# Attention half steps issued tile by tile, with value products in halves, on one Trainium2 core

## Chip, cores and metric

The kernel runs on one core of one Trainium2 chip. The metric is the device time in microseconds, median of the runs of one launch each; the lower the better.

## What is computed

Two layers over x of shape (4, 512, 256), with a context of the same shape. Layer 0: gated cross-attention (16 heads of 16, softmax over 512 context rows), then a top-2 mixture of 8 experts. Layer 1: gated cross-attention again, then a feed-forward block with quantised activations and ternary weights. Cut to the attention and the two blocks after it:

```python
q = split_heads(LN(x) @ Wq.T + bq); k = split_heads(ctx @ Wk.T + bk); v = split_heads(ctx @ Wv.T + bv)
w = softmax(einsum('bhqd,bhkd->bhqk', q, k) / sqrt(16))
x = x + tanh(g_xattn[l]) * (merge(einsum('bhqk,bhkd->bhqd', w, v)) @ Wo.T + bo)
# layer 0: x = x + tanh(g_ffn[0]) * sum over the 2 best experts of wf_e * (LN(x) @ We)
# layer 1: x = x + tanh(g_ffn[1]) * bitlinear(gelu(bitlinear(LN(x), w1)), w2)
```

## The kernel before

Eight passes follow one another, `p` = 0 to 7: four batches of layer 0, then the same four of layer 1. A pass has 16 attention steps `G` (four heads of a group times four tiles of 128 context rows), and a step has two half steps, the slots of the program. `table()` writes one list of work for the whole kernel, slot by slot; each engine walks that list and issues only what it owns, so the list fixes every engine's order. Nothing is decided at run time but the waits on semaphores.

In a slot stand first the tiles of attention, then one "piece" of other work from `work_table()` (a projection, an expert, a part of the feed-forward block), so that TensorE has something to do beside the softmax. The tiles of attention are:

- `S` (`s_pair`, L754): two scores of 128 query rows by 512 context rows, heads r = 0 and 1, six steps ahead of their use. They serve only for the row maxima, which VectorE takes (`maxima`, L1171) from three PSUM buffers `psS`. Head 0 lies on partitions 0 to 63 of the stacks `qs` and `ks`, head 1 on 64 to 127, so the two matmuls use different row halves of the array.
- `T` (`t_pair`, L768): the same scores transposed, with the maxima as two further contraction rows, for the same two heads, into the two buffers of `psT`. ScalarE takes both with one exponential of 1024 columns (`exps`, L991) into `pt`. The next `t_pair` waits for that exponential.
- `PV` (`pv_quad`, L782): in every second slot, four matmuls of 512 columns into `psO`, one for each head of the group, side by side in four strips of 32 columns of the array, fp32. Each is two MATMULs in the trace, so a quad shows x8. It takes the step before, G-1.

The maxima of four steps are copied and split on GpSimd (`m`, L648, L651), transposed on TensorE (`MT`, L791), copied by ScalarE (`mt_`, L1007) and put into rows of `qs` with four small DMAs on the queue of SyncE (`max_rows`, L531). `SPLIT` projects keys or queries (L707); ScalarE writes it twice (`qf` L938, `parts` L939), GpSimd subtracts (L574), and the parts go through DRAM into `qs` and `ks`. `ME` is an expert (L843 to L845, six matmuls in a slot, read by VectorE at L1302). `F1` (L879), `HT` (L889) and `F2` (L897) are the feed-forward block, and GELU (L1042) reads `F1` from `psT` and `psS`; `VV` (L727) is the value projection. After the last pass comes a tail in which one batch goes alone through `OP`, the layer norm, `XB` (L858), `F1`, `HT` and `F2`.

## Time and profile before

| | us |
|---|---|
| median of 3 runs (lowest, highest) | 766.89 (765.59, 769.69) |
| the profiled run's own time | 766.51 |
| its span in the trace | 764.7 |
| outside the span | 1.8 |
| PE busy in the span | 676.7 (88%) |
| DVE busy | 530.5 (69%) |
| ACT busy | 446.8 (58%) |
| POOL busy | 167.0 (22%) |

PE is TensorE, DVE VectorE, ACT ScalarE, POOL GpSimd and SP SyncE, whose busy time is not counted. The ends of matmuls are modelled: a lone matmul of 512 columns is shown with 0.39 to 0.50 us, while the next one of the same kind starts after 0.23. Starts are therefore the better measure. The passes take 85.1, 90.1, 88.8, 88.9, 88.8, 82.1, 76.1 and 78.1 us, counted from first exponential to first exponential; ahead of them lie 46.9 us, behind them 39.8.

### The profile page before, as it was taken

What the parts mean: (1) busy time and instruction counts of PE and PEld (TensorE: products, weight loads), DVE (VectorE), ACT (ScalarE), POOL (GpSimd) and SP (SyncE); (2) the same over time, 40 slices, a digit from 0 to 9 for tenths busy, and PEclk for the clock granted to TensorE, in tenths of its full rate; (3) what the DMA queues carried; (4) which work ended last, traced back from release to release, by engine and by line L of the source; (5) the groups of instructions that cost most, each with busy time, mean ns of one, the idle gap of its engine ahead of it and who ended that gap; (6) DMA issues with size and microseconds to landing.
All of it is one profiled execution on the core that took longest, in us unless ns stands there. A gap on an engine that the chain in (4) does not pass through costs nothing.

```text
span 764.7 us, 10140 instructions
## 1 busy us (share of the span) xinstructions
PE 676.7 (88%) x3550; PEld 323.6 (42%) x3554; DVE 530.5 (69%) x1138; ACT 446.8 (58%) x572; POOL 167.0 (22%) x302
## 2 busy tenths in 40 slices
PE   4799999998999999998999989998889789987746
PEld 2433333344544445444554445443344344432324
DVE  3467876578886688868787688864786768775234
ACT  2227666773346633664336734468776778568746
POOL 6325222630010310121101410113210311021132
PEclk9769999999999999999999999999999999969987
DMA  7848578512120601123220321216032312200000
GB/s 239 230 117 317 180 232 267 158 34 52 42 43 29 166 18 26 46 108 84 43 43 30 122 47 42 43 70 207 10 83 64 94 39 64 43 2 9 21 0 28
DMA packets 39922, 66.74 MB, mean 87 GB/s; under 512 B 6080, under 2 KB 14784, under 8 KB 39616
## 3 DMA queue, kind: packets, MB, share of 16 engines
q1 hardware_dynamic: 39024, 65.57, 30.0%
q8 instruction: 28, 0.46, 0.3%
q10 hardware_dynamic: 848, 0.53, 0.2%
q14 instruction: 22, 0.18, 0.1%
HBM read 38.29 MB, written 27.26 MB: 86 GB/s over the span
## 4 chain that ended last, share of the span: by engine, by line
PE 56%; DVE 14%; ACT 12%; issue 9%; POOL 6%; DMA 2%; SPq 0%; POOLq 0%; DVEq 0%; ACTq 0%
PE psO L782 10%; PE psS L754 7%; PE psX L707 7%; DVE mx L1171 6%; PE psT L768 6%; PE psX L843 5%; PE psX L819 4%; ACT pt L991 4%; PE psX L844 4%; PE psX L845 4%; PE psX L727 3%; ACT qf L938 2%; DVE xs L1302 2%; POOL parts L574 2%; ACT parts L939 2%
## 5 line engine op out<-in xcount | busy, mean ns | idle before, releaser
L991 ACT ACTIVATE pt<-psT 128x1024 f32<-128x1024 f32 x256 | 261.8, 1023 | 217.1 <-PE psT L768 214.7
L1171 DVE TENSOR_REDUCE mx<-psS 128x1 f32<-128x512 f32 x512 | 325.1, 681 | 87.4 <-PE psS L754 86.1
L754 PE MATMUL psS<-ks,qs 48*128 48x512 f32 x512 | 153.8, 516 | 18.9 <-DVE mx L1171 13.2
L782 PE MATMUL psO<-pt,vg 128*32 128x512 f32 x1024 | 140.4, 621 | 0.1
L768 PE MATMUL psT<-qs,ks 50*128 50x512 f32 x512 | 118.2, 431 | 9.6 <-ACT pt L991 8.2
L754 PEld LDWEIGHTS psS<-ks,qs 48*128 48x128 f32 x512 | 61.0, 191 | 138.2 <-issue 72.3
L1302 DVE SCALAR_TENSOR_TENSOR xs<-psX,coef,xs 128x256 f32<-128x256 f32 x128 | 61.8, 483 | 31.8 <-PE psX L845 28.5
L574 POOL TENSOR_TENSOR parts<-qf,parts 128x512 fp32r<-128x512 f32 x32 | 40.8, 1275 | 158.7 <-ACT parts L939 158.7
L768 PEld LDWEIGHTS psT<-qs,ks 50*128 50x128 f32 x512 | 52.2, 189 | 29.4 <-ACT pt L991 25.8
L843 PE MATMUL psX<-moeh,xh 128*128 128x512 f32 x128 | 57.1, 446 | 5.3 <-DVE xs L1302 5.3
L844 PE MATMUL psX<-moel,xh 128*128 128x512 f32 x128 | 50.7, 396 | 0.0
L845 PE MATMUL psX<-moeh,xl 128*128 128x512 f32 x128 | 50.2, 392 | 0.0
L843 PEld LDWEIGHTS psX<-moeh,xh 128*128 128x128 f32 x128 | 23.9, 187 | 43.9 <-DVE xs L1302 23.8
L707 PE MATMUL psX<-ctxb,wk 128*128 128x512 f32 x64 | 34.4, 667 | 7.7 <-DMA wk<-in_Wk 7.7
L648 POOL CAST mp<-mx 128x16 fp32r<-128x16 f32 x32 | 6.4, 199 | 158.6 <-DVE mx L1171 157.7
L948 ACT ACTIVATE xn<-xs,lnw 128x256 f32<-128x256 f32 x60 | 31.8, 591 | 14.2 <-POOL lnw L610 14.1
L663 POOL TENSOR_SCALAR hh<-hh,am 128x1024 f32<-128x1024 f32 x16 | 18.0, 1123 | 95.2 <-DVE am L1343 95.2
L782 PEld LDWEIGHTS psO<-pt,vg 128*32 128x32 f32 x1024 | 20.3, 108 | 43.5 <-issue 42.5
L707 PE MATMUL psX<-xnt,wq 128*128 128x512 f32 x64 | 32.2, 630 | 1.3 <-ACT xnt L961 0.8
L819 PE MATMUL psX<-wo,ont 128*128 128x256 f32 x128 | 31.6, 391 | 0.8 <-ACT ont L984 0.8
L1100 DVE BATCH_NORM_STATS2 st<-xs 128x6 f32<-128x256 f32 x64 | 26.4, 413 | 7.4 <-DMA xs<-in_x 6.7
L1125 DVE TENSOR_TENSOR vg<-psX,bvb 128x512 f32<-128x512 f32 x16 | 11.0, 691 | 29.1 <-PE psX L727 29.1
(128 smaller groups left out, 748.9 us busy)
## 6 DMA issues: line engine op xcount, KB each, us to landing
ks<-kd SPq DMA_DIRECT2D x64, 192.0 KB, 3.7
qs<-qd SPq DMA_DIRECT2D x64, 192.0 KB, 4.5
kd<-parts SPq DMA_DIRECT2D x16, 512.0 KB, 3.1
qd<-parts SPq DMA_DIRECT2D x16, 512.0 KB, 2.7
kd<-parts SPq DMA_DIRECT2D x16, 256.0 KB, 3.8
qd<-parts SPq DMA_DIRECT2D x16, 256.0 KB, 3.7
ctxb<-in_ctxT SPq DMA_DIRECT2D x7, 512.0 KB, 3.5
xs<-in_x SPq DMA_DIRECT2D x4, 512.0 KB, 6.4
```

The source lines that it names most:

```text
L574: g.tensor_tensor(parts[:, i % 2, 1, :].bitcast(F32R), qf[:, i % 2, :], parts[:, i % 2, 0, :], ALU.subtract).then_inc(p_split, 1)
L707: i = mm(o, w[:, k, c * P:(c + 1) * P], src[:, k, :], start=k == 0, stop=k == NC - 1)
L754: mm(psS[:, i % 3, :], qs[at:at + KR, 2 * g + a, k * P:(k + 1) * P], ks[at:at + KR, 2 * g + a, :], start=True, stop=True).then_inc(pe_s, 1)
L768: i = mm(psT[:, r, :], ks[at:at + KR + MP, 2 * g + half, k * P:(k + 1) * P], qs[at:at + KR + MP, 2 * g + half, :], start=True, stop=True)
L782: i = mm(psO[32 * j:32 * j + 32, :], vg[:, p % 2, k, g * GH + j, :], pt[:, s % RING, j, :], start=k == 0, stop=k == NT - 1, tile_position= ...
L819: i = mm(o[:, t * D:(t + 1) * D], ont[:, k, tt * P:(tt + 1) * P], wo[l][:, k, :], start=k == 0, stop=k == NC - 1)
L843: mm(o, xh[:, k, tok], moeh[:, k, at], start=k == 0, stop=False)
L844: mm(o, xh[:, k, tok], moel[:, k, at], start=False, stop=False)
L845: i = mm(o, xl[:, k, tok], moeh[:, k, at], start=False, stop=k == NC - 1)
L991: a(pt[:, G % RING, 2 * half:2 * half + 2, :], psT[:], ACT.Exp, scale=SCALE).then_inc(a_exp, 1)
L1171: v.tensor_reduce(mx[:, w // GH % 2, r, col:col + 1], psS[:, i % 3, :], AX.X, ALU.max).then_inc(v_max, 1)
L1302: v.scalar_tensor_tensor(out=xs[:, b, t, :], in0=o[:, k * D:(k + 1) * D], scalar=coef[:, t, e:e + 1], in1=xs[:, b, t, :], op0=ALU.mult, op ...
```

## The change

The half step is issued tile by tile. Where a slot had S, S, T, T and then perhaps a whole PV, it has T of head 0, S of head 1, half a PV, T of head 1, S of head 0. The PV of a step is cut into two halves of 256 columns, one in each slot; the first of each four (k = 0, which starts the accumulation) stays whole, in the second slot. Each T has an exponential of its own, 512 columns, and a T waits only for the exponential before the last. The four DMAs of the maxima become two of two rows each.

Besides: in the layer-1 bursts of F1 both VV stand around the four F1, not between them; the two first query splits are subtracted on VectorE straight from PSUM, without the `qf` copy; BOB and the BIAS additions come later; and in the tail a new `BUSY` issues matmuls whose result nobody reads (29, 4, 4 and 9 of them) between the steps of the last batch. The diff, cut to these:

```diff
-    put(lead, 24, ("BOB", ()))
-    put(lead, 25, ("BIAS", (0, 0)))
+    put(lead, 31, ("BOB", ()))
...
+    for b in range(B):
+        put(0, 5 + 8 * b, ("BIAS", (b, 0)))
...
-            for t in range(NT):
-                put(p, 16, ("F1", (t,)))
-                if p < NP - 1 and t in (1, 2):
-                    put(p, 16, ("VV", (p + 1, t - 1)))
+            burst = [("F1", (t,)) for t in range(NT)]
+            if p < NP - 1:
+                burst = [("VV", (p + 1, 0))] + burst + [("VV", (p + 1, 1))]
+            put(p, 16, *burst)
...
-    put(NP, 5, ("XQ", (0, 2)), ("LNN", (b, 2, 4)), ("XI", (0, 2)), ("XB", (0, 2)), ("XQ", (2, 4)), ("XI", (2, 4)))
-    put(NP, 5, ("F1", (0,)), ("XB", (2, 4)), ("F1", (1,)), ("F1", (2,)), ("F1", (3,)))
+    put(NP, 4, ("BUSY", (29,)))
+    put(NP, 5, ("XQ", (0, 2)), ("LNN", (b, 2, 4)), ("XI", (0, 2)), ("XB", (0, 2)), ("BUSY", (4,)), ("XQ", (2, 4)), ("XI", (2, 4)))
+    put(NP, 5, ("F1", (0,)), ("XB", (2, 4)), ("BUSY", (4,)), ("F1", (1,)), ("F1", (2,)), ("F1", (3,)),
+        ("BUSY", (9,)))
...
-        if 0 <= w < NP * H:
-            out.append(("S", (w, half)))
-        if 0 <= G < NP * H:
-            out.append(("T", (G, half)))
-        if half == 1 and 0 <= G - 1 < NP * H:
-            out.append(("PV", (G - 1,)))
-            if G % GH == 0:
-                out.append(("OE", ()))
+        for r in range(2):
+            if 0 <= G < NP * H:
+                out.append(("T", (G, half, r)))
+            if 0 <= w < NP * H:
+                out.append(("S", (w, half, 1 - r)))
+            if r == 0 and 0 <= G - 1 < NP * H and (half or (G - 1) % GH):
+                out.append(("PV", (G - 1, half)))
+        if 0 <= G - 1 < NP * H and half == 1 and G % GH == 0:
+            out.append(("OE", ()))
...
+        def by_dve(i):
+            return i in (split_no["Q", 0, 0], split_no["Q", 0, 1])
+        def dve_parts(i):
+            return sum(by_dve(k) for k in range(i))
+        def pool_parts(i):
+            return i - dve_parts(i)
+        def act_parts(i):
+            return 2 * i - dve_parts(i)
...
                 for k in range(MP):
-                    for half in range(2):
-                        row, src = HALF * half + KR + k, k * GH * NT + half * 2 * NT
-                        sp.dma_start(qs[row:row + 1, 2 * g:2 * g + 2, :].bitcast(F32)
-                                     .rearrange("p h (t q) -> p (h t) q", q=P),
-                                     mt[src:src + 2 * NT, i % 2, :]).then_inc(d_m[i % 2], 16)
+                    sp.dma_start(qs[KR + k:HALF + KR + k + 1:HALF, 2 * g:2 * g + 2, :].bitcast(F32)
+                                 .rearrange("p h (t q) -> p (h t) q", q=P),
+                                 mt[k * GH * NT:(k + 1) * GH * NT, i % 2, :]).then_inc(d_m[i % 2], 16)
...
-            def s_pair(w, half):
+            def s_tile(w, half, r):
                 g, a, k = w // GH % NG, w % GH // 2, 2 * (w % 2) + half
-                if w % GH == 0 and half == 0:
+                i, at = n("S"), HALF * r
+                if i % (4 * GH) == 0:
                     if due(dq[g], 32 * (w // H + 1)):
                         pe.wait_ge(dq[g], 32 * (w // H + 1))
                     if due(dk[g], 32 * (w // H + 1)):
                         pe.wait_ge(dk[g], 32 * (w // H + 1))
-                for r in range(2):
-                    at, i = HALF * r, n("S", 2, r)
-                    if due(v_max, i - 2):
-                        pe.wait_ge(v_max, i - 2)
-                    if due(a_f1, n("F1")):
-                        pe.wait_ge(a_f1, n("F1"))
-                    mm(psS[:, i % 3, :], qs[at:at + KR, 2 * g + a, k * P:(k + 1) * P], ks[at:at + KR, 2 * g + a, :],
-                       start=True, stop=True).then_inc(pe_s, 1)
-            def t_pair(G, half):
+                if due(v_max, i - 2):
+                    pe.wait_ge(v_max, i - 2)
+                if due(a_f1, n("F1")):
+                    pe.wait_ge(a_f1, n("F1"))
+                mm(psS[:, i % 3, :], qs[at:at + KR, 2 * g + a, k * P:(k + 1) * P], ks[at:at + KR, 2 * g + a, :],
+                   start=True, stop=True).then_inc(pe_s, 1)
+            def t_tile(G, half, r):
                 g, k, no = G // GH % NG, G % GH, G // GH
+                at = HALF * r
                 if k == 0 and half == 0:
-                    if due(d_m[no % 2], 64 * (no // 2 + 1)):
-                        pe.wait_ge(d_m[no % 2], 64 * (no // 2 + 1))
-                if due(a_exp, n("T")):
-                    pe.wait_ge(a_exp, n("T"))
+                    if due(d_m[no % 2], 32 * (no // 2 + 1)):
+                        pe.wait_ge(d_m[no % 2], 32 * (no // 2 + 1))
+                if due(a_exp, n("T") - 1):
+                    pe.wait_ge(a_exp, n("T") - 1)
                 if due(a_f1, n("F1") - 1):
                     pe.wait_ge(a_f1, n("F1") - 1)
-                for r in range(2):
-                    at = HALF * r
-                    i = mm(psT[:, r, :], ks[at:at + KR + MP, 2 * g + half, k * P:(k + 1) * P],
-                           qs[at:at + KR + MP, 2 * g + half, :], start=True, stop=True)
-                i.then_inc(pe_t, 1)
-            def pv_quad(s):
+                mm(psT[:, r, :], ks[at:at + KR + MP, 2 * g + half, k * P:(k + 1) * P],
+                   qs[at:at + KR + MP, 2 * g + half, :], start=True, stop=True).then_inc(pe_t, 1)
+            def pv_quad(s, half):
                 p, g, k = s // H, s // GH % NG, s % GH
-                if due(a_exp, 2 * (s + 1)):
-                    pe.wait_ge(a_exp, 2 * (s + 1))
+                if due(a_exp, 4 * (s + 1)):
+                    pe.wait_ge(a_exp, 4 * (s + 1))
                 if due(v_vv, 2 * (p + 1)):
                     pe.wait_ge(v_vv, 2 * (p + 1))
                 if k == 0:
                     if due(a_oe, n("OE")):
                         pe.wait_ge(a_oe, n("OE"))
+                at = slice(half * S // 2, (half + 1) * S // 2) if k else slice(0, S)
                 for j in range(GH):
-                    i = mm(psO[32 * j:32 * j + 32, :], vg[:, p % 2, k, g * GH + j, :], pt[:, s % RING, j, :],
-                           start=k == 0, stop=k == NT - 1, tile_position=(0, 32 * j))
-                i.then_inc(pe_pv, 1)
+                    i = mm(psO[32 * j:32 * j + 32, at], vg[:, p % 2, k, g * GH + j, :], pt[:, s % RING, j, at],
+                           start=k == 0, stop=half == 1 and k == NT - 1, tile_position=(0, 32 * j))
+                if half:
+                    i.then_inc(pe_pv, 1)
...
+            def keep_busy(k):
+                if due(a_oe, n("OE")):
+                    pe.wait_ge(a_oe, n("OE"))
+                if due(v_quant, 16):
+                    pe.wait_ge(v_quant, 16)
+                for i in range(k):
+                    mm(psO[:], identb[:], w1q[:, 0, 0:S], start=True, stop=True)
...
-            def exps(G, half):
+            def exps(G, half, r):
                 if due(pe_t, n("T") + 1):
                     act.wait_ge(pe_t, n("T") + 1)
                 if due(pe_pv, G - RING + 1):
                     act.wait_ge(pe_pv, G - RING + 1)
-                a(pt[:, G % RING, 2 * half:2 * half + 2, :], psT[:], ACT.Exp, scale=SCALE).then_inc(a_exp, 1)
+                a(pt[:, G % RING, 2 * half + r, :], psT[:, r, :], ACT.Exp, scale=SCALE).then_inc(a_exp, 1)
...
+            def split(what, p, c):
+                i = n("SPLIT")
+                if not by_dve(i):
+                    return
+                if due(pe_split, i + 1):
+                    dve.wait_ge(pe_split, i + 1)
+                if due(a_split, act_parts(i + 1)):
+                    dve.wait_ge(a_split, act_parts(i + 1))
+                v.scalar_tensor_tensor(out=parts[:, i % 2, 1, :].bitcast(F32R), in0=bank(), scalar=bqc[:, 0, c:c + 1],
+                                       in1=parts[:, i % 2, 0, :], op0=ALU.add, op1=ALU.subtract).then_inc(v_split, 1)
...
-            def maxima(w, half):
+            def maxima(w, half, r):
+                i = n("S")
                 col = w % GH // 2 * NT + 2 * (w % 2) + half
-                if w % GH == 0 and half == 0:
+                if i % (4 * GH) == 0:
                     if due(p_m, 2 * (w // GH - 1)):
                         dve.wait_ge(p_m, 2 * (w // GH - 1))
-                for r in range(2):
-                    i = n("S", 2, r)
-                    if due(pe_s, i + 1):
-                        dve.wait_ge(pe_s, i + 1)
-                    v.tensor_reduce(mx[:, w // GH % 2, r, col:col + 1], psS[:, i % 3, :], AX.X, ALU.max
-                                    ).then_inc(v_max, 1)
+                if due(pe_s, i + 1):
+                    dve.wait_ge(pe_s, i + 1)
+                v.tensor_reduce(mx[:, w // GH % 2, r, col:col + 1], psS[:, i % 3, :], AX.X, ALU.max).then_inc(v_max, 1)
```

How this moves TensorE's instructions is seen at three places. In the expert stretch of a layer-0 pass, before (psS is a score, psT a transposed score, psO a value product, psX a piece; here an expert):

```order
L845 MATMUL psX<-moeh,xl 128x512
L754 MATMUL psS<-ks,qs 128x512 x2
L768 MATMUL psT<-qs,ks 128x512 x2
L782 MATMUL psO<-pt,vg 32x512 x4
L843 MATMUL psX<-moeh,xh 128x512
```

and in the changed kernel:

```order
L869 MATMUL psX<-moeh,xl 128x512
L791 MATMUL psT<-qs,ks 128x512
L778 MATMUL psS<-ks,qs 128x512
L805 MATMUL psO<-pt,vg 32x256 x4
L791 MATMUL psT<-qs,ks 128x512
L778 MATMUL psS<-ks,qs 128x512
L867 MATMUL psX<-moeh,xh 128x512
```

One run of four score tiles has become two runs of two with a value product of half the columns between them, and this now stands in both slots of a step.

In the feed-forward part of a layer-1 pass, where a slot has no piece, before (L897 is F2, L889 is HT):

```order
L897 MATMUL psX<-w2q,hqt 128x256 x8
L754 MATMUL psS<-ks,qs 128x512 x2
L768 MATMUL psT<-qs,ks 128x512 x2
L754 MATMUL psS<-ks,qs 128x512 x2
L768 MATMUL psT<-qs,ks 128x512 x2
L782 MATMUL psO<-pt,vg 32x512 x4
L889 MATMUL psX<-identb,hq 128x128 x8
```

and in the changed kernel:

```order
L921 MATMUL psX<-w2q,hqt 128x256 x8
L791 MATMUL psT<-qs,ks 128x512
L778 MATMUL psS<-ks,qs 128x512
L805 MATMUL psO<-pt,vg 32x256 x4
L791 MATMUL psT<-qs,ks 128x512
L778 MATMUL psS<-ks,qs 128x512
L791 MATMUL psT<-qs,ks 128x512
L778 MATMUL psS<-ks,qs 128x512
L805 MATMUL psO<-pt,vg 32x256 x4
L791 MATMUL psT<-qs,ks 128x512
L778 MATMUL psS<-ks,qs 128x512
L913 MATMUL psX<-identb,hq 128x128 x8
```

The eight score tiles stood together; now they are three runs with two value products between.

In the F1 burst of a layer-1 pass, before (L879 is F1, L727 is VV):

```order
L768 MATMUL psT<-qs,ks 128x512 x2
L879 MATMUL psT<-w1q,xit 128x512 x4
L879 MATMUL psS<-w1q,xit 128x512 x4
L727 MATMUL psX<-wv1,ctxb 128x256 x4
L879 MATMUL psT<-w1q,xit 128x512 x4
L727 MATMUL psX<-wv1,ctxb 128x256 x4
L879 MATMUL psS<-w1q,xit 128x512 x4
L754 MATMUL psS<-ks,qs 128x512 x2
```

and in the changed kernel:

```order
L778 MATMUL psS<-ks,qs 128x512
L752 MATMUL psX<-wv1,ctxb 128x256 x4
L903 MATMUL psT<-w1q,xit 128x512 x4
L903 MATMUL psS<-w1q,xit 128x512 x4
L903 MATMUL psT<-w1q,xit 128x512 x4
L903 MATMUL psS<-w1q,xit 128x512 x4
L752 MATMUL psX<-wv1,ctxb 128x256 x4
L791 MATMUL psT<-qs,ks 128x512
```

One VV now stands ahead of the first F1, the other behind the last.

Over the whole program, TensorE's list has these unbroken runs of one kind: score tiles 240 before and 421 after, value products 127 and 223, everything else 200 and 200.

## Rows read from the trace of the kernel before

**Rows 1.** Windows of four stretches: us, busy us (instructions) by engine, clock, DMA.

```profile
core 0: us, PE busy (x) PEld busy (x) DVE busy (x) ACT busy (x) POOL busy (x), PEclk, DMA share, GB/s
...
310.90:399.80 88.90, 85.11 (x453) 43.48 (x454) 68.11 (x156) 46.10 (x62) 13.92 (x29) 1.00 0.22 60
...
570.70:646.80 76.10, 66.72 (x399) 30.42 (x394) 55.58 (x111) 55.76 (x66) 12.93 (x26) 1.00 0.26 69
...
735.00:764.70 29.70, 15.67 (x87) 9.07 (x88) 12.57 (x38) 17.16 (x20) 9.90 (x23) 0.71 0.05 18
...
280.00:302.90 22.90, 22.68 (x118) 11.82 (x116) 18.60 (x39) 8.83 (x10) 0.42 (x2) 1.00 0.17 36
```

**Rows 2.** Timeline of PE, expert stretch: start, length, instruction.

```profile
301.21 0.50 PE L754 MATMUL psS<-ks,qs 48*128 48x512 f32 x2
301.55 0.40 PE L768 MATMUL psT<-qs,ks 50*128 50x512 f32 x2
301.88 1.06 PE L782 MATMUL psO<-pt,vg 128*32 128x512 f32 x8
302.87 0.50 PE L843 MATMUL psX<-moeh,xh 128*128 128x512 f32 x1
303.20 0.39 PE L844 MATMUL psX<-moel,xh 128*128 128x512 f32 x1
303.44 0.39 PE L845 MATMUL psX<-moeh,xl 128*128 128x512 f32 x1
```

**Rows 3.** Waits of PE over the span: us in total, times, longest.

```profile
PE psS L754 <- DVE mx L1171: 13.2, 24, 1.4
PE psT L768 <- ACT pt L991: 8.2, 25, 1.1
PE psX L791 <- POOL mp L651: 8.1, 15, 1.3
```

**Rows 4.** Timeline of a layer-1 pass, no piece between the slots.

```profile
571.89 0.45 PE L768 MATMUL psT<-qs,ks 50*128 50x512 f32 x2
...
572.38 1.02 ACT L991 ACTIVATE pt<-psT 128x1024 f32<-128x1024 f32 x1 [0.68 <-PE psT L768]
...
573.45 0.50 PE L768 MATMUL psT<-qs,ks 50*128 50x512 f32 x2
```

**Rows 5.** Groups of ACT by form: busy us, mean ns, idle before.

```profile
L991 ACT ACTIVATE pt<-psT 128x1024 f32<-128x1024 f32 x256 | 261.8, 1023 | 217.1 <-PE psT L768 214.7
...
L999 ACT ACTIVATE osb<-psO 128x512 f32<-128x512 f32 x32 | 19.1, 598 | 1.2 <-PE psO L782 1.2
```

**Rows 6.** Timeline of PE, F1 burst of the first layer-1 pass.

```profile
532.20 0.81 PE L879 MATMUL psT<-w1q,xit 128*128 128x512 bf16 x3 [1.35 <-ACT pt L991]
...
533.71 1.89 PE L727 MATMUL psX<-wv,ctxb 128*128 128x256 f32 x8
535.43 1.03 PE L879 MATMUL psT<-w1q,xit 128*128 128x512 bf16 x4
...
540.26 0.50 PE L754 MATMUL psS<-ks,qs 48*128 48x512 f32 x2 [1.21 <-ACT hh L1042]
```

**Rows 7.** Timeline of the start: query split, and the small operations of the lead.

```profile
19.98 1.27 POOL L574 TENSOR_TENSOR parts<-qf,parts 128x512 fp32r<-128x512 f32 x1 [3.97 <-ACT parts L939]
20.35 0.69 ACT L938 ACTIVATE qf<-psX,bqc 128x512 f32<-128x512 f32 x1 [0.45 <-PE psX L707]
...
22.08 0.69 DVE L1125 TENSOR_TENSOR vg<-psX,bvb 128x512 f32<-128x512 f32 x1 [5.34 <-PE psX L727]
...
36.42 0.60 DVE L1087 TENSOR_SCALAR bob<-bob,gt 128x256 f32<-128x256 f32 x2
...
42.03 2.84 SPq L531 DMA_DIRECT2D qs<-mt  x4
```

**Rows 8.** Timeline of PE in the tail.

```profile
746.27 1.86 PE L879 MATMUL psS<-w1q,xit 128*128 128x512 bf16 x4 [1.36 <-ACT xit L1031]
747.93 1.54 PE L879 MATMUL psT<-w1q,xit 128*128 128x512 bf16 x4
```

51 lines of the change are left out of this document (31 added, 20 removed).

## The prediction, made before the changed kernel was run

> **What bounds the kernel now.** I read the windows by pass first, then TensorE's timeline inside a pass, then its waits, and last the start and the tail. The windows show PE as the fullest engine everywhere: 85.1 of 88.9 us in a layer-0 pass, 66.7 of 76.1 in a layer-1 pass, with VectorE next (68.1 and 55.6). In the expert stretch of a layer-0 pass PE is busy for 22.68 of 22.90 us while VectorE has 18.6 and ScalarE 8.8 [rows 1]. A busy PE proves nothing alone, since the ends of matmuls are modelled, so the starts must tell. They do: in the expert stretch experts follow one another every 0.23 us, and each group of score tiles and each value product starts at a fixed distance from what stands before it [rows 2]. Nothing is waited for there; the stretch is TensorE's own instruction stream. Elsewhere there are waits, but small ones: of the 764.7 us span, scores wait 13.2 us for the maxima, transposed tiles 8.2 us for the exponential, the transposes of the maxima 8.1 us for GpSimd [rows 3]. That is what a finer interleaving can win at most, apart from the ends. So the question is what the new order costs TensorE itself.
>
> **What a change of kind costs on TensorE.** From the starts [rows 2]: the first pair of score tiles takes 0.34 us to the next pair (301.21 to 301.55), against 0.23 from expert to expert (303.20 to 303.44), though a pair with its two row halves runs together and is as long as one matmul. The 0.11 more is a weight load that nothing hides, for the first expert after a value product starts 0.33 before the second as well. The last pair takes 0.33 to the value product (301.55 to 301.88): 0.10 more than 0.23, the emptying of the array before another kind of tile. So a run of score tiles costs 0.21 us beside its columns, however short. The value product takes 0.99 us (301.88 to 302.87). Its columns: eight fp32 matmuls of 256 columns of the value projection take 1.72 us (533.71 to 535.43), 0.215 each [rows 6], so 512 columns twice are 0.86, and 0.13 is what a run of value products costs beside them.
>
> **The sum of the new order.** In the program's lists the runs of score tiles go from 240 to 421, those of value products from 127 to 223; the columns are the same. 181 × 0.21 = 38 us and 96 × 0.13 = 12.5 us: **+50 us**, if TensorE never waits. For one step of the expert stretch this is 2 × 0.21 + 0.13 = 0.55 us, where the value product is whole 0.21; with eight such steps in each of the four passes, 4 × (6 × 0.55 + 2 × 0.21) = 15 us fall where nothing is waited for [rows 1, 2], and these I hold for certain. The other 35 fall where waits lie between.
>
> A rule of the Trainium skill bears on this, in TensorEngine Tiling (Array Packing), section Key Properties: changing the tiling mode, not just the tile, makes TensorE drain. Score tiles use half the rows and all columns, value products all rows and a strip of columns, so the rule speaks against each new alternation. By the drain alone (0.10 of the row's 0.21) the sum would be 28 to 31 us; the row has the unhidden load too and decides.
>
> **What it wins back in the passes.** Waits first. A transposed pair now waits for the whole exponential of the pair before: 571.89, exponential 572.38 to 573.40, next pair 573.45, thus 1.56 us a slot at least [rows 4]. With single tiles a T needs only the exponential before the last, and I take that wait as gone. The row of 8.2 us in 25 waits is short by the modelled ends (0.40 shown against 0.23, so 0.17 a wait [rows 2, 3]): 12.5 us. The waits on maxima are 13.2 + 24 × 0.17 = 17 us, of which the reductions themselves, whose number and size stay, keep some: half, 8 us, is my choice between none and all. Together **−20 us** (between 0 and 29). Then, TensorE's added time falls in part into waits for others that end no later for it: the row of 8.1 us in 15 waits for the split maxima (10.7 with the ends), and those of the feed-forward block. I take **−8 us** (0 to 18).
>
> ScalarE: 256 exponentials of 1023 ns become 512; a copy of 512 columns out of PSUM takes 598 ns [rows 5], so its busy time grows by 512 × 0.598 − 261.8 = 44 us (5.6 in a pass). A layer-1 pass has 55.8 of 76.1 busy [rows 1], and 61 of 76 is still under TensorE; cost on the path 0, and if that cover is gone, up to 15 us in three passes. A value product's first half now stands right behind the next T and S and needs the last exponential of its step. Where a piece lies between (1.4 us for an expert), that is ready; where none does, the second T must end (0.33), be taken (0.60), and TensorE has 0.6 us of tiles in between: 0.3 us of new wait in a minority of steps, within the choice above. Behind it on PE stand T, S and the piece, for which both other engines wait.
>
> **F1 bursts.** From the first F1 (532.20, first of it slightly earlier) to the next score tile (540.26) go 8.1 us, with a wait of 1.35 ahead of it and 1.21 behind it [rows 6]. The VV of 1.72 us put ahead fills the first wait, and the other one ends after the last GELU; four GELUs then run at ScalarE's pace. I count 1.85 us for each of two bursts, **−3.7** (0 to −5).
>
> **The start.** The query split loses the `qf` copy (0.69, of which 0.59 on the path) and GpSimd's 1.27 us, and gains a VectorE operation like the 0.69 us addition from PSUM: −1.2 us. BOB (0.60) leaves the chain of maxima. Four small DMAs take 2.84 us to issue, two half of that, but the lead's score tiles cover most of it: at most 0.2 on the path there, elsewhere nothing, since the rows are wanted three steps later; if that cover were gone it would be 1.4 [rows 7]. BIAS moved costs nothing: it is wanted a pass later. **−2.0**.
>
> **The tail.** The clock there is 0.71 in the mean [rows 1], and F1 takes 1.66 us from its first matmul to the next F1 (746.27 to 747.93), 0.42 each where full clock gives half of it [rows 8]. Idle TensorE stood before the drop; the added matmuls fill such gaps. If the clock stays up, four F1, HT and F2 are worth 3 to 5 us; the fillers themselves can stand in the way of an XB or F1 by up to 0.9. **−3** (+1 to −5).
>
> **The sum.** 50 − 20 − 8 − 3.7 − 2.0 − 3 = +13.3 us. Against the profiled run's own 766.5 (span 764.7 and 1.8 around it) this is 779.8; its time is 0.4 below the median of 766.9, so I say **780**.
>
> **The rivals.**
> 1. *Forecast, chance 0.55*: slower, TensorE pays for the alternation and gets less than half back in waits. Its own range is 771 to 795.
> 2. *The waits were the larger part, and it is faster (0.20).* Outside the expert stretches the loop T, exponential, T with 1.56 us a slot is what sets the pace of light slots [rows 4]; if breaking it hides all 35 us of added stream there and takes the 20 us of waits as well, then 15 − 20 − 8.7 = −14: **752**. It decides where the some 96 steps outside the expert stretches shorten by over 0.07 us each (6.3 / 96). For it: the loop is seen in layer 1. Against it: the row of these waits is small, and PE is busy 0.88 of even that pass [rows 1, 3].
> 3. *ScalarE or VectorE becomes the bound as well (0.18).* With 44 us more on ScalarE, and value products behind the last exponential, waits are not won but moved: 50 − 8.7 − 8 + 0 to 50 − 8.7 + 15 × 0.3 = 33 to 46, hence 800 to **812**; nearer 800, since ScalarE is busy 9 of 23 us in the expert stretch [rows 1].
> 4. *It cancels out (0.07)*: within 0.5% of 766.9, if 41 us are won back.
>
> **How the numbers follow.** Likeliest 780. The bounds of the choices: nothing won back in the passes, 766.5 + 50 − 8.7 = 808; everything, 766.5 + 50 − 29 − 18 − 10 = 760. Leaving about a tenth on each side, I give 757 to 802. A difference of 0.5% (3.8 us) is about what can be told from none here. Slower by more: 0.55 + 0.18 = 0.73; within: 0.07; faster: 0.20.
>
> **What would show it.** In the changed profile's expert stretch: T and S start together, the half product 0.43 us after them, the next T 0.56 us later, the piece 0.43 after that; a step 0.55 longer than before. Layer-0 passes of 92 to 95 us. Layer-1 passes near the old ones. The wait of T for the exponential under 3 us. In the tail a clock near 1. It is wrong if the half product starts 0.23 after the tiles (no emptying), if T and S do not run together (then worse, near 30 us more), or if the light steps fall well below their old length.

## The result, and the profile after

| | before | changed |
|---|---|---|
| median of 4 runs each, us (lowest, highest) | 768.29 (765.59, 769.99) | 802.3 (798.79, 811.35) |
| the profiled run's own time, its span | 766.51, 764.7 | 799.24, 797.4 |
| mean granted clock of the profiled run | 0.960 | 0.955 |
| PE, DVE, ACT busy, us | 676.7, 530.5, 446.8 | 729.4, 541.1, 468.9 |
| ahead of the first exponential, us | 46.9 | 44.7 |
| passes 0 to 7, us | 85.1 90.1 88.8 88.9 88.8 83.8 78.1 74.4 | 91.4 93.2 97.0 94.3 96.9 84.4 78.7 79.5 |
| PE idle in the eight passes, us | 54.2 | 43.7 |
| behind the last pass, us | 39.8 | 37.2 |

The changed kernel takes 1.0431 times as long (95% interval 1.0391 to 1.047). All medians here are of all runs, while the ratios leave out single runs far above the fastest of their kernel (here that of 811.35 us, at a mean clock of 0.935, without which the median is 799.24). The forecast was 780 with a range up to 802: the direction came true, the size did not. The start and the tail are shorter in these two profiles, and every pass is longer: passes 0 to 4, among them all with experts, by 3.1 to 8.2 us, the last three by 0.6, 0.6 and 5.1. Counted from first exponential to first exponential, passes 6 and 7 of the kernel before begin at 572.38 [rows 4] and 650.48 us, not at 570.7 and 646.8; so passes 5 to 7 took the times above, and not 82.1, 76.1 and 78.1.

The windows of the changed kernel, in the order of [rows 1] with pass 3 first, then pass 6 (to within 2 us), the tail, and an expert stretch:

```profile
core 0: us, PE busy (x) PEld busy (x) DVE busy (x) ACT busy (x) POOL busy (x), PEclk, DMA share, GB/s
326.30:420.60 94.30, 91.20 (x554) 46.67 (x556) 68.92 (x156) 49.61 (x93) 13.89 (x29) 0.98 0.22 57
601.50:679.20 77.70, 70.18 (x501) 32.64 (x504) 57.65 (x113) 58.66 (x98) 12.96 (x26) 1.00 0.25 69
767.70:797.40 29.70, 22.21 (x139) 11.71 (x140) 15.06 (x44) 16.85 (x20) 10.54 (x24) 1.00 0.05 18
392.00:414.90 22.90, 22.90 (x137) 11.97 (x135) 17.61 (x36) 9.17 (x17) 0.42 (x2) 1.00 0.17 36
```

No other engine became the bound: ScalarE has 49.6 of 94.3 and 58.7 of 77.7 us. The clock of the tail went from 0.71 to 1.00. In the expert stretch the records leave PE no gap, and its timeline is the place to check the price of a change of kind:

```profile
395.48 0.39 PE L869 MATMUL psX<-moeh,xl 128*128 128x512 f32 x1
395.81 0.50 PE L791 MATMUL psT<-qs,ks 50*128 50x512 f32 x1
395.81 0.50 PE L778 MATMUL psS<-ks,qs 48*128 48x512 f32 x1
396.24 0.64 PE L805 MATMUL psO<-pt,vg 128*32 128x256 f32 x8
396.81 0.50 PE L791 MATMUL psT<-qs,ks 50*128 50x512 f32 x1
396.81 0.49 PE L778 MATMUL psS<-ks,qs 48*128 48x512 f32 x1
397.23 0.50 PE L867 MATMUL psX<-moeh,xh 128*128 128x512 f32 x1
...
398.82 0.50 PE L791 MATMUL psT<-qs,ks 50*128 50x512 f32 x1
```

`T` and `S` start together; 0.43 us later the half product, 0.57 after that the next tiles, 0.42 after them the expert. A slot takes 3.01 us (395.81 to 398.82), a step 6.02 against 5.5 before. The forecast had 0.43, 0.56, 0.43 and 0.55 for the step.

The waits of PE that answer to [rows 3] (us in total, times, longest):

```profile
PE psT L791 <- ACT pt L1024: 13.7, 31, 1.6
PE psX L867 <- DVE xs L1344: 8.2, 4, 2.1
...
PE psX L815 <- POOL mp L673: 4.2, 7, 0.8
PE psO L805 <- ACT pt L1024: 4.2, 11, 0.7
...
PE psS L778 <- DVE mx L1214: 0.9, 2, 0.6
```

Scores no longer wait for maxima: 13.2 us became 0.9. Transposed tiles wait more for the exponential, 13.7 against 8.2, the product has a wait of its own, 4.2, and the first expert of a slot waits 8.2 for VectorE, in 4 long waits behind the router, where it was 5.3 in 12. The three rows of [rows 3] sum to 29.5 us; the waits that stand in their places here (13.7, 4.2, 4.2, 0.9) sum to 23.0. The interleaving took one wait away and fed another. In all, PE was idle for 10.5 us less in the passes, where the forecast wanted 20 and more.

The exponential by form, beside [rows 5]:

```profile
L1024 ACT ACTIVATE pt<-psT 128x512 f32<-128x512 f32 x512 | 293.5, 597 | 237.2 <-PE psT L791 234.6
```

597 ns each, the 598 of the copy that the forecast took. The start, beside [rows 7]:

```profile
19.51 0.75 DVE L1171 SCALAR_TENSOR_TENSOR parts<-psX,bqc,parts 128x512 fp32r<-128x512 f32 x1 [4.83 <-ACT parts L972]
```

The split ends at 20.26 where GpSimd ended at 21.25 (19.98 + 1.27), 1.0 us earlier. How long the whole start takes differs more than that among kernels that all have these edits: 43.7 to 47.8 us in their profiles, with a granted clock of 0.84 there in the shortest (f3) and 0.79 in the longest (e4), against 46.9 at 0.81 before.

### The profile page after: what moved, and what is told of

Read it like the earlier page. It is cut to its first block, busy times and chain, and to the rows that moved or that the text cites. A ratio compares the mean times of both kernels' runs of the same rounds, so it can differ in the third digit from the quotient of the medians.

```text
span 797.4 us, 11959 instructions
## 1 busy us (share of the span) xinstructions
PE 729.4 (91%) x4363; PEld 351.5 (44%) x4368; DVE 541.1 (68%) x1140; ACT 468.9 (59%) x826; POOL 164.3 (21%) x300
## 4 chain that ended last, share of the span: by engine, by line
PE 69%; ACT 13%; DVE 9%; POOL 5%; issue 4%; DMA 0%; SPq 0%; DVEq 0%; POOLq 0%; ACTq 0%
PE psT L791 19%; PE psO L805 14%; PE psX L732 7%; PE psX L867 5%; PE psX L843 4%; PE psX L869 4%; PE psX L868 4%; PE psX L752 4%; DVE mx L1214 3%; ACT pt L1024 3%; ACT xn L981 2%; PE psX L921 2%; ACT hq L1086 2%; ACT qf L971 2%; ACT parts L972 1%
## 5 line engine op out<-in xcount | busy, mean ns | idle before, releaser
L1024 ACT ACTIVATE pt<-psT 128x512 f32<-128x512 f32 x512 | 293.5, 597 | 237.2 <-PE psT L791 234.6
L1214 DVE TENSOR_REDUCE mx<-psS 128x1 f32<-128x512 f32 x512 | 335.1, 683 | 100.4 <-PE psS L778 98.7
L791 PE MATMUL psT<-qs,ks 50*128 50x512 f32 x512 | 246.3, 499 | 14.2 <-ACT pt L1024 13.7
L778 PE MATMUL psS<-ks,qs 48*128 48x512 f32 x512 | 249.7, 512 | 1.7 <-DVE mx L1214 0.9
L791 PEld LDWEIGHTS psT<-qs,ks 50*128 50x128 f32 x512 | 94.2, 188 | 207.7 <-issue 148.1
L805 PE MATMUL psO<-pt,vg 128*32 128x256 f32 (+1 forms) x1792 | 162.4, 435 | 4.8 <-ACT pt L1024 4.2
L778 PEld LDWEIGHTS psS<-ks,qs 48*128 48x128 f32 x512 | 96.0, 192 | 10.7 <-DVE mx L1214 7.8
L1344 DVE SCALAR_TENSOR_TENSOR xs<-psX,coef,xs 128x256 f32<-128x256 f32 x128 | 61.9, 483 | 42.6 <-PE psX L869 39.8
L805 PEld LDWEIGHTS psO<-pt,vg 128*32 128x32 f32 x1792 | 35.8, 109 | 64.8 <-issue 47.5
L981 ACT ACTIVATE xn<-xs,lnw 128x256 f32<-128x256 f32 x60 | 31.7, 590 | 15.5 <-POOL lnw L632 15.5
L752 PE MATMUL psX<-wv,ctxb 128*128 128x256 f32 x128 | 35.3, 423 | 0.8 <-DVE parts L1171 0.8
L613 POOL TENSOR_SCALAR lnw<-mv 128x4 f32<-128x4 f32 (+1 forms) x17 | 3.9, 229 | 134.0 <-DVE mv L1138 133.4
```

What stands on the lines that cost most here:

```text
L752: i = mm(o[:, t * D:(t + 1) * D], ctxb[:, p % 2, k, (2 * half + t) * P:(2 * half + t + 1) * P], wv[l][:, k, :], start=k == 0, stop=k == NC ...
L778: mm(psS[:, i % 3, :], qs[at:at + KR, 2 * g + a, k * P:(k + 1) * P], ks[at:at + KR, 2 * g + a, :], start=True, stop=True).then_inc(pe_s, 1)
L791: mm(psT[:, r, :], ks[at:at + KR + MP, 2 * g + half, k * P:(k + 1) * P], qs[at:at + KR + MP, 2 * g + half, :], start=True, stop=True).then ...
L805: i = mm(psO[32 * j:32 * j + 32, at], vg[:, p % 2, k, g * GH + j, :], pt[:, s % RING, j, at], start=k == 0, stop=half == 1 and k == NT - 1 ...
L1024: a(pt[:, G % RING, 2 * half + r, :], psT[:, r, :], ACT.Exp, scale=SCALE).then_inc(a_exp, 1)
L1214: v.tensor_reduce(mx[:, w // GH % 2, r, col:col + 1], psS[:, i % 3, :], AX.X, ALU.max).then_inc(v_max, 1)
```

## The experiments

The question was where the 22 us between 780 and 802 come from. My theory: the price of the alternation was right, and the value products and second tiles that were moved between the pairs did not win waits but shifted them to the exponentials. The rivals: the price is larger outside the expert stretches than its rows say; the other edits (start, burst, tail, DMAs) cost instead of helping; the maxima, taken late, hold up the scores. In the diffs, - is the changed kernel's code unless another is named. "Runs" below are runs of tiles and of value products in the program's lists: 240 and 127 before, 421 and 223 changed. All ratios are to the kernel before.

### The other edits without the new order

**e4** keeps the start, burst, tail and joined DMAs, and restores the order S, S, T, T, the exponential of 1024 columns, and whole products (240 and 127 runs).

```
         for r in range(2):
+            if 0 <= w < NP * H:
+                out.append(("S", (w, half, r)))
+        for r in range(2):
             if 0 <= G < NP * H:
                 out.append(("T", (G, half, r)))
-            if 0 <= w < NP * H:
-                out.append(("S", (w, half, 1 - r)))
-            if r == 0 and 0 <= G - 1 < NP * H and (half or (G - 1) % GH):
-                out.append(("PV", (G - 1, half)))
+        if 0 <= G - 1 < NP * H and half:
+            out.append(("PV", (G - 1, half)))
...
+                if r == 0:
+                    return
-                a(pt[:, G % RING, 2 * half + r, :], psT[:, r, :], ACT.Exp, scale=SCALE).then_inc(a_exp, 1)
+                a(pt[:, G % RING, 2 * half:2 * half + 2, :], psT[:], ACT.Exp, scale=SCALE).then_inc(a_exp, 1)
```

> The order and the exponentials of before the change (S, S, T, T, one exponential for both T, whole value product), with the other parts of the change: two DMAs for the maxima, start, F1 bursts, tail. It prices those parts: 768.3 - 2.0 - 3.7 - 3 = 759.6 if each is worth what the prediction gave it. The difference from the kernel with T, S, T, S in one run is what single tiles and single exponentials win in waits: 9 us by theory A, nothing or a loss by theory B.

Measured: 763.89 (10 runs), ratio 0.9941 (0.9919 to 0.9963). The other edits together are worth 4.5 us, not the forecast's 8.7, and they cost nothing. The whole loss, 802.3 − 763.9 = 38 us, is the new order's with its exponentials, whose price in runs is 50.5.

**e7** is the changed kernel without the `BUSY` matmuls of the tail.

```
-    put(NP, 4, ("BUSY", (29,)))
-    put(NP, 5, ("XQ", (0, 2)), ("LNN", (b, 2, 4)), ("XI", (0, 2)), ("XB", (0, 2)), ("BUSY", (4,)), ("XQ", (2, 4)), ("XI", (2, 4)))
-    put(NP, 5, ("F1", (0,)), ("XB", (2, 4)), ("BUSY", (4,)), ("F1", (1,)), ("F1", (2,)), ("F1", (3,)),
-        ("BUSY", (9,)))
+    put(NP, 5, ("XQ", (0, 2)), ("LNN", (b, 2, 4)), ("XI", (0, 2)), ("XB", (0, 2)), ("XQ", (2, 4)), ("XI", (2, 4)))
+    put(NP, 5, ("F1", (0,)), ("XB", (2, 4)), ("F1", (1,)), ("F1", (2,)), ("F1", (3,)))
```

> The changed kernel without the added matmuls of the tail. The prediction gave them with the clock 3 us; the profile of the changed kernel shows the tail 2.6 us shorter than before. So 805, with the granted clock of the tail low again. If the fillers stand in the way of F1 as much as they help: 802, no difference.

Measured: 800.36 (5 runs), ratio 1.0426 (1.0389 to 1.0464), no different from the changed kernel. Its last 29.7 us:

```profile
773.40:803.10 29.70, 15.22 (x88) 8.08 (x88) 12.72 (x38) 17.04 (x20) 9.99 (x23) 0.70 0.05 18
```

The fillers do what they say (clock 0.70 to 1.00, and the tail 39.7 to 37.2 us), but the medians do not show those 2.5 us. With 5 runs against 7 they could hardly: the means, 801.0 and 800.6 (the changed kernel with f4, below), are known to about 1 us each.

### The order, one part at a time

**e1** leaves the order of tiles and puts the product whole into the second slot, still between the pairs (326 and 128 runs).

```
-            if r == 0 and 0 <= G - 1 < NP * H and (half or (G - 1) % GH):
+            if r == 0 and 0 <= G - 1 < NP * H and half:
...
-                at = slice(half * S // 2, (half + 1) * S // 2) if k else slice(0, S)
+                at = slice(0, S)
```

> The changed kernel with the value product whole again, in the second slot of a step, still between the two pairs of tiles (T, S, value product, T, S). TensorE's list has 326 runs of score tiles and 128 of value products (240 and 127 before the change, 421 and 223 with it). Theory A, the price is per run on TensorE (0.21 us a run of tiles, 0.13 a run of value products) and the waits give back some 13 us: 768.3 - 4.8 (start and tail) - 12.7 + 18 = 769, thus 33 us under the changed kernel. Theory B, the loss sits in new waits (a first half that needs the last exponential, ScalarE with 512 exponentials): this kernel removes the first half but keeps the exponentials, so it falls by less than 15, to some 790.

Measured: 789.56 (4 runs), ratio 1.0308 (1.023 to 1.0386). Better than the changed kernel by some 12 us, where the runs taken out were priced at 95 × 0.21 + 95 × 0.13 = 32. Its waits give part of the reason: PE is idle for 55.2 us in its passes, 43.7 in the changed kernel's, and of this 6 us lie in the wait for the exponential, 13.7 there:

```profile
PE psT L791 <- ACT pt L1024: 19.7, 46, 1.6
```

**e2** keeps the halves and lets T, S, T, S stand together, the half product behind them (256 and 222 runs). **e3** does the same with whole products (240 and 127). e2, from the changed kernel:

```
-            if r == 0 and 0 <= G - 1 < NP * H and (half or (G - 1) % GH):
-                out.append(("PV", (G - 1, half)))
+        if 0 <= G - 1 < NP * H and (half or (G - 1) % GH):
+            out.append(("PV", (G - 1, half)))
```

e3, from e2:

```
-        if 0 <= G - 1 < NP * H and (half or (G - 1) % GH):
+        if 0 <= G - 1 < NP * H and half:
...
-                at = slice(half * S // 2, (half + 1) * S // 2) if k else slice(0, S)
+                at = slice(0, S)
```

> The changed kernel with both pairs of tiles in one run (T, S, T, S) and the half value products behind them, in both slots. 256 runs of tiles, 222 of value products. Theory A: 16 us for the runs, 768.3 - 4.8 - 12.7 + 16 = 767. Theory B (new waits for exponentials behind the halves): halves and single exponentials are all still there, so it stays above 790.

> The changed kernel with T, S, T, S in one run and the value product whole behind them in the second slot: the runs of before the change (240 and 127), with single exponentials, two DMAs, and the changed start, bursts and tail. Theory A: 768.3 - 4.8 - 12.7 = 751, the fastest of all. Theory B (single exponentials cost on ScalarE): above 765.

Measured: e2 758.11 (4 runs), ratio 0.986 (0.9822 to 0.9898); e3 759.3 (4 runs, scattered from 751.4 to 764.9), ratio 0.9809 (0.9754 to 0.9865). Two lines of order turn a kernel 4.3% slower than before into one 1.4% faster. e2's timeline in an expert stretch:

```profile
388.21 0.50 PE L791 MATMUL psT<-qs,ks 50*128 50x512 f32 x1
388.21 0.49 PE L778 MATMUL psS<-ks,qs 48*128 48x512 f32 x1
388.55 0.40 PE L791 MATMUL psT<-qs,ks 50*128 50x512 f32 x1
388.55 0.40 PE L778 MATMUL psS<-ks,qs 48*128 48x512 f32 x1
388.88 1.07 PE L805 MATMUL psO<-pt,vg 128*32 128x512 f32 x8
...
391.46 0.50 PE L791 MATMUL psT<-qs,ks 50*128 50x512 f32 x1
```

The second pair follows 0.34 us after the first, as in the kernel before [rows 2]: what a second run would add (0.10 of emptying and 0.11 of load) is not paid. The product here is a whole one, the first of its group.

**e6** is e4 with single exponentials, **e11** is e4 with half products behind the tiles in both slots and the exponential of 1024 columns kept (256 and 222 runs). e6, from e4:

```
-                if due(a_exp, n("T") // 2):
-                    pe.wait_ge(a_exp, n("T") // 2)
+                if due(a_exp, n("T") - 1):
+                    pe.wait_ge(a_exp, n("T") - 1)
...
-                if r == 0:
-                    return
```

and e11, from e4 (which also has the line `at = slice(half * S // 2, ...)` of the changed kernel back):

```
-        if 0 <= G - 1 < NP * H and half:
+        if 0 <= G - 1 < NP * H and (half or (G - 1) % GH):
```

> The order of before (S, S, T, T, whole value product) with single exponentials of 512 columns, and the changed start, bursts, tail and DMAs. The kernel with these parts but the one exponential of 1024 columns took 763.9; T, S, T, S in one run with single exponentials 759.3. If the single exponentials do the work, about 759; if the order T, S, T, S does (a T earlier in its slot), 764.

> The order of before with one exponential for both T, and the value product in halves behind the tiles in both slots (256 and 222 runs, 16 us of price), with the changed start, bursts, tail and DMAs. Halves and single exponentials together gave 758.1, whole products and single exponentials 759.3, thus the halves cost 1 us less than nothing where the price says 16 more: they win back some 16 us of waits. If the halves do this alone: 763. If they need the single exponentials (their first half waits for the last exponential, which comes 0.4 us later when it takes 1024 columns): the price stays, 775 to 785.

Measured: e6 763.02 (10 runs), ratio 0.9947 (0.9926 to 0.9967); e11 769.26 (10 runs), ratio 1.0037 (1.0014 to 1.006). Single exponentials alone are 0.9 us below e4, and no different from it by the ratios. Halves alone cost 5.4 (7.4 by the ratios), where 16 × 0.21 + 95 × 0.13 = 15.7 more is in the stream: 8 to 10 of the price does not arrive. Both together with T, S, T, S (e2, run again as f3: 760.13) are 3.8 below e4 with the same 15.7: 19.5 does not arrive. This is the size of the forecast's 20, reached without the alternation. Not all of it is waits: PE's idle time in the passes is 50.0 us in e4, 43.6 in e6, 41.1 in e11, 38.6 in e2 and 37.1 in f3, so at most 13 us less.

e6 and e3 differ in the order of the tiles alone, S, S, T, T and T, S, T, S, and their waits say what that order does, e6 first:

```profile
PE psS L779 <- DVE mx L1215: 14.6, 25, 1.4
...
PE psT L792 <- ACT pt L1025: 1.4, 2, 0.7
```

```profile
PE psT L791 <- ACT pt L1024: 12.0, 30, 1.6
...
PE psS L778 <- DVE mx L1214: 5.4, 15, 0.5
```

Single exponentials do take the wait of T away (8.6 us in e4, 1.4 in e6), as forecast. Putting a T first in the slot brings it back and takes the wait for the maxima away instead.

**e9** and **e10** take the two pairs apart by kind: S, S, half product, T, T, and T, T, half product, S, S (413 runs of tiles in both). The edit of e9; e10 has the two loops exchanged:

```
         for r in range(2):
-            if 0 <= G < NP * H:
-                out.append(("T", (G, half, r)))
             if 0 <= w < NP * H:
                 out.append(("S", (w, half, 1 - r)))
-            if r == 0 and 0 <= G - 1 < NP * H and (half or (G - 1) % GH):
-                out.append(("PV", (G - 1, half)))
+        if 0 <= G - 1 < NP * H and (half or (G - 1) % GH):
+            out.append(("PV", (G - 1, half)))
+        for r in range(2):
+            if 0 <= G < NP * H:
+                out.append(("T", (G, half, r)))
```

> The changed kernel with both scores ahead of the half value product and both transposed tiles behind it (S, S, half product, T, T): 413 runs of tiles and 223 of value products, as many as in the changed kernel. With the two pairs together ahead of the half products the time was 758.1, which is 44 us under the changed kernel, where the price of 165 runs is 35. The other 9 need a cause. Theory L, the late last score: VectorE takes its maxima in order, and all that it owes the piece (experts, router, norms) stands behind the late one. Then this order, with both scores early, is 4 to 9 us under the changed kernel: 793 to 798. Theory X, the late last transposed tile: exponentials come later and the next half product and T wait; then this order is slower than the changed kernel, 805 to 812.

> The mirror image: both transposed tiles ahead of the half product, both scores behind it (T, T, half product, S, S): 413 and 222 runs. Theory L: both maxima are late, so it stays at the changed kernel's time or above, 802 to 810. Theory X: both exponentials are early, 793 to 798. Only the array's price (theory A): both orders within 3 us of the changed kernel.

Measured: e9 834.42 (4 runs), ratio 1.0855 (1.0804 to 1.0907); e10 806.37 (4 runs), ratio 1.0517 (1.0472 to 1.0562). The first waits of the two, e9 first (its profiled run, 843.37 us, had a mean clock of 0.923, that of e10 0.962):

```profile
PE psO L806 <- ACT pt L1025: 24.2, 39, 1.2
```

```profile
PE psT L792 <- ACT pt L1025: 7.8, 13, 1.4
```

The price of both is (413 − 240) × 0.21 + 95 × 0.13 = 48.7 over e4, or 812.6. e10 stays 6 below it; e9, with its transposed tiles last, adds 22 to it. PE is idle for 54.0 us in the passes of e9 and 28.7 in those of e10. So it is the transposed tile that must be early, for the product waits for its exponential. A rival of mine, that late scores and their maxima are what hurts, falls: e10 has the scores last and is 28 us the better one.

**e5** is the changed kernel's order with one exponential of 1024 columns for a pair, taken after the second tile.

```
-                if due(a_exp, n("T") - 1):
-                    pe.wait_ge(a_exp, n("T") - 1)
+                if due(a_exp, n("T") // 2):
+                    pe.wait_ge(a_exp, n("T") // 2)
...
             def exps(G, half, r):
+                if r == 0:
+                    return
```

> The changed kernel's order, but one exponential of 1024 columns for both transposed tiles, as before the change; the first T of a slot then waits for the whole pair. It prices the single exponentials in this order. If the loop T, exponential, T is what they break: slower than the changed kernel by 5 to 12 us, 807 to 814. If ScalarE's 32 us more of busy time is what hurts: faster, 790 to 798.

Measured: 928.23 (5 runs), ratio 1.2064 (1.2008 to 1.2119), by far the largest effect of the study.

```profile
PE psT L791 <- ACT pt L1026: 87.7, 104, 1.2
```

With the product between the two tiles, the pair's exponential starts 1.0 us later and the next first tile waits for all of it, 104 times. The waits shown are 88 us and the loss beside the changed kernel is 126; the mean granted clock of the profiled run, 940.88 us, was 0.847, and 0.862 in the run at the median. TensorE was granted 1.2 GHz for 287 us of the span, 72 in the changed kernel, so the clock has a part in the loss that can be larger than that of the waits. In the alternating order the single exponential is not a gain but a necessity.

### Where the alternation costs

**f1** alternates (product between the pairs) only in slots that hold an expert, **f2** only in the others; in the remaining slots both are e2. **f3** is e2 again and **f4** the changed kernel again, on the same chip. The edit of f1 from e2; f2 has `not any` in its first line:

```
+        alt = any(k == "ME" for k, _ in work.get(slot, []))
...
-        if 0 <= G - 1 < NP * H and (half or (G - 1) % GH):
-            out.append(("PV", (G - 1, half)))
+            if r == (0 if alt else 1) and 0 <= G - 1 < NP * H and (half or (G - 1) % GH):
+                out.append(("PV", (G - 1, half)))
```

> Tiles together with half products behind them everywhere, but in the slots that hold an expert the changed kernel's order (T, S, half product, T, S). 312 runs of tiles against 256. Theory P, only the price of 0.21 us a run, exact where nothing waits: 12 us over the kernel with tiles together. Theory Q, the price a run is really 0.27 (44 us over 165 runs): 15 us. Theory R, the order in an expert slot is hidden: 0.

> The mirror image: the changed kernel's order in all slots without an expert, tiles together in those with one. 365 runs of tiles against 256. Theory P with the rest in waits and clock of the light slots: 23 + 9 = 32 us over the kernel with tiles together. Theory Q: 29. If the light slots' waits hid part of the price, as the prediction said: 5 to 15. The two kernels' surpluses should add up to that of the changed kernel.

> Tiles together (T, S, T, S), half products behind them, again, as the lower end on this chip: 758 as before; the granted clock 0.97.

> The changed kernel again, as the upper end on this chip: 802, the granted clock near 0.955.

| | runs of tiles | median, us (runs) | ratio (95%) | over f3 | price over f3 |
|---|---|---|---|---|---|
| f3 | 256 | 760.13 (10) | 0.9891 (0.9857 to 0.9926) | | |
| f1 | 312 | 777.3 (4) | 1.0123 (1.0048 to 1.0198) | 17.2 | 56 × 0.21 = 11.8 |
| f2 | 365 | 783.33 (4) | 1.0244 (1.0151 to 1.0337) | 23.2 | 109 × 0.21 = 22.9 |
| f4 | 421 | 800.64 (4) | 1.0443 (1.0375 to 1.0512) | 40.5 | 165 × 0.21 = 34.7 |

The two parts add up: 17.2 + 23.2 = 40.4. The profiles say what they are made of. These windows are the eight passes of f3, f1, f2 and f4; what PE's busy time leaves of the first number is its idle time, 37.1, 37.4, 43.3 and 43.4 us:

```profile
43.70:724.70 681.00, 643.89 (x4117) 311.10 (x4114) 493.51 (x1047) 426.73 (x784) 137.59 (x242) 0.97 0.29 82
```

```profile
44.70:739.00 694.30, 656.91 (x4115) 316.82 (x4113) 493.00 (x1045) 431.24 (x784) 137.32 (x242) 0.96 0.28 81
```

```profile
44.30:744.60 700.30, 657.03 (x4115) 315.83 (x4113) 500.78 (x1046) 435.09 (x784) 137.98 (x242) 0.97 0.28 80
```

```profile
43.70:756.20 712.50, 669.08 (x4116) 321.24 (x4114) 502.11 (x1047) 439.34 (x784) 137.61 (x242) 0.97 0.27 79
```

With an expert in the slot (f1) PE waits no longer than in f3. In the other slots (f2) PE's busy time grows by 13.1 us for 109 runs, 0.12 each and not 0.21, and its idle time by 6.2. That the median is 23.2 above f3's where 22.9 was priced is thus luck in part: the array costs less there than its price, and new waits make up for it. Slot by slot, from first T to first T, the traces say the same. Where neither has a wait nor the lower clock, a slot of f1 with an expert and one more run than in f3 is 0.19 us longer (50 slots), a slot of f2 with another piece and one more run 0.11 (69 slots). The first waits of f3, then of f1 and of f2:

```profile
PE psT L791 <- ACT pt L1024: 10.5, 22, 1.2
...
PE psX L867 <- DVE xs L1344: 6.3, 4, 1.6
PE psS L778 <- DVE mx L1214: 5.8, 13, 0.6
```

```profile
PE psT L792 <- ACT pt L1025: 8.9, 18, 0.7
PE psX L868 <- DVE xs L1345: 8.5, 4, 2.1
```

```profile
PE psT L792 <- ACT pt L1025: 15.5, 35, 1.6
...
PE psO L806 <- ACT pt L1025: 4.2, 11, 0.7
...
PE psS L779 <- DVE mx L1215: 0.9, 2, 0.5
```

f1 has no more waits for exponentials than f3; what grew is the wait behind the router, from 1.6 to 2.1 us at the longest. f2 has the changed kernel's waits: against f3 it lost 4.9 us of waits for maxima and took on 5.0 of T for the exponential and most of 4.2 of the product. So the slots without an expert are where the interleaving meets waits at all, and there it exchanges one for more of another. f1's timeline of PE at the router in pass 3, the fourth pass:

```profile
369.89 0.66 PE L824 MATMUL psX<-identf,osb 128*128 128x128 f32 x4
...
372.68 0.50 PE L868 MATMUL psX<-moeh,xh 128*128 128x512 f32 x1 [2.14 <-DVE xs L1345]
...
374.49 0.79 PE L792 MATMUL psT<-qs,ks 50*128 50x512 f32 x1
```

The changed kernel has the same place:

```profile
377.15 0.50 PE L867 MATMUL psX<-moeh,xh 128*128 128x512 f32 x1 [2.13 <-DVE xs L1344]
...
379.10 0.79 PE L791 MATMUL psT<-qs,ks 50*128 50x512 f32 x1
379.11 0.79 PE L778 MATMUL psS<-ks,qs 48*128 48x512 f32 x1
379.83 1.93 PE L805 MATMUL psO<-pt,vg 128*32 128x512 f32 x8
```

After an idle of 2.1 us and a few experts, tiles are 0.79 us long and the product starts 0.73 after them, against 0.50 and 0.43 above: the clock was granted at 1.2 GHz. The windows of pass 3, f1 first, then f3:

```profile
321.90:416.20 94.30, 91.27 (x552) 46.86 (x551) 68.13 (x156) 48.79 (x94) 13.90 (x29) 0.96 0.22 57
```

```profile
317.00:405.80 88.80, 86.10 (x550) 44.92 (x548) 67.96 (x156) 47.56 (x94) 13.92 (x29) 1.00 0.23 61
```

f1's pass is 5.5 us longer than f3's. A quarter of 11.8, 2.9 us, is the price of its runs, 0.5 the longer wait; the trace has 6.8 us of it at 1.2 GHz, where up to 3.4 us of work are lost. Over all passes f1's trace has 56 us at 1.2 GHz and f3's 44, and the mean clock of all runs is 0.9565 in f1 and 0.9664 in f3. Runs of one kernel differ by some 0.5 us for each 0.001 of it (last section), so the clock is worth about 5 us: that is an estimate, but it is the 5.4 us by which f1 exceeds its price, and the idle time leaves no room for waits. For f4, at 0.955, the same estimate gives 5.7; the two profiled runs of f4 and f3, at 0.961 and 0.962, differ by 31.5 us in the passes, less than the price of 34.7. Whether the order lowers the clock through its longer waits, one of which stands ahead of the stretch above, is not shown.

### The burst and the tail, again on the better order

**e12** is e2 with the value projections between the F1s as before, **e13** is e12 without `BUSY` (the same edit as e7). e12, from e2:

```
-            burst = [("F1", (t,)) for t in range(NT)]
-            if p < NP - 1:
-                burst = [("VV", (p + 1, 0))] + burst + [("VV", (p + 1, 1))]
-            put(p, 16, *burst)
+            for t in range(NT):
+                put(p, 16, ("F1", (t,)))
+                if p < NP - 1 and t in (1, 2):
+                    put(p, 16, ("VV", (p + 1, t - 1)))
```

> The kernel with both pairs together and half products behind them (758.1), with the F1 bursts as before the change (VV between the F1). The prediction gave the new burst 3.7 us: 762. If TensorE's idling among the F1 costs the clock what the shorter burst gains: 758, no difference.

> The same, with the old bursts and without the added matmuls of the tail. Without them the changed kernel took 800.4 against 802.3, so they won nothing there where I had given them 3 us. If that holds here: as the kernel with old bursts alone, within 2 us. If the prediction's size holds: 3 us above it.

Measured: e12 766.86 (10 runs), ratio 0.9988 (0.9958 to 1.0018); e13 767.86 (10 runs), ratio 1.0017 (0.9989 to 1.0046). The moved value projections shorten passes 5 and 6 by 3.2 and 1.2 us in the profiles (83.7 and 76.6 against e2's 80.5 and 75.4), where 3.7 was forecast for the two. But only 2.0 us of this is idle time of PE (12.1 to 10.1); e12 has a mean clock of 0.96 in pass 5 and e2 1.00. The medians of e12 and f3 differ by 6.7, their mean clocks by 0.006, some 3 us by the same estimate. The fillers shorten the tail from 40.2 to 37.2 us, and the medians differ by 1.0, the means by 1.7, known to about 1.3; 3 us are not excluded.

## Why the prediction failed in its size

**The price of the alternation: right where TensorE waits for nothing, too high elsewhere.** 0.21 for a run of tiles and 0.13 for a run of products, read from a few starts, held in the expert stretch (a step is 0.52 longer for a forecast 0.55, and the slots of f1 0.19 for 0.21). In slots with another piece a run cost 0.11. From e4 to f4, whose traces have nearly the same time at 1.2 GHz in the passes (48 and 47 us), PE's busy time grows by 36.2 us, where the price is 50.5.

**"What it wins back in the passes": here the prediction failed.** It took −20 for waits on exponentials and maxima, and −8 for added time that falls into other waits.

- The −20 was 6.6: PE's idle time in the passes is 50.0 us in e4 and 43.4 in f4. This is the term that was mis-sized, and by 13 us the largest.
- The step that failed is "With single tiles a T needs only the exponential before the last, and I take that wait as gone". It goes with single exponentials behind S, S (e6, 1.4 us); with a T first in the slot it comes back (12.0 in e3, 10.5 in f3) and is largest with the product between the pairs (13.7, and 4.2 more of the product itself). The wait for maxima went almost wholly (0.9), where half was counted. The mistake stands again in the text at "0.3 us of new wait in a minority of steps, within the choice above". Where this is made stronger the time runs away (e9 +22 over the price, e5 +126 over the changed kernel).
- The −8 was not too large: 50.5 − 36.2 = 14 us of the price did not lengthen PE's busy time. This division is an estimate, for the modelled ends of matmuls can hide short waits in busy time.
- The order's sum in the passes is 36.2 − 6.6 = 29.6 us in the profiles, where 22 was forecast. The medians of e4 and f4 differ by 36.8. The rest goes with the clock, a term that the prediction had for the tail alone: its mean is 0.9636 in the runs of e4 and 0.955 in those of f4, some 4 us by the estimate above, and the last 3 are within the scatter of the runs.

**ScalarE: right in kind.** 597 ns each; the exponentials' busy time rose by 293.5 − 261.8 = 31.7 us and all of ScalarE's by 22.1, where I said 44 (512 × 0.597 is 305.7, so successive exponentials overlap in the records). It did not become the bound. Rival 3 (waits moved, not won; 800 to 812) had the time and half of the cause: products do wait behind the last exponential, but a full ScalarE the windows don't show.

**The other edits: half.** −8.7 forecast, −4.5 measured (e4). By the profiles the tail came as forecast (−2.6 for 3). For the burst, e2 shows 2.0 us less idle time of PE, where 3.7 was forecast, beside a clock that differs. The start's 2.0 is not shown: one step of it ended 1.0 earlier, while e4, with all of the start's edits, took 47.8 us to its first exponential, 0.9 more than the kernel before. That alone accounts for much of what is missing in e4.

**The rivals.** Faster (752) fell: outside the expert slots the slots took 19 us longer in sum. Only the 58 without any piece shortened, by 14 us; the 133 with another piece lengthened by 33. Cancelling out fell. The forecast's own points of test came true except three: layer-0 passes of 92 to 95 were 91.4 to 97.0, the last pass was 5.1 above its old length, and the waits of T for the exponential, which I wanted under 3 us, are 13.7. The third was the sign that its reason was wrong.

**The better kernel.** T, S, T, S together and half products behind (e2, f3) takes 758.1 and 760.1 us, ratio 0.986 and 0.9891: it beats both.
